# Zero matmuls ahead of TensorE's waits, and rounds counted in registers, in a graph network kernel on one core

## What is computed

```python
x = _layernorm(x + gat(x, src, dst))         # 4 heads: softmax over a node's edges, then a weighted sum
x = _layernorm(x + deviation(x, src, dst))   # standard deviation of the messages of a node
x = _layernorm(x + gine(x, edge_attr, ...))  # sum of x[src] + edge_attr @ We, then an MLP
x = _layernorm(x + sage(x, ...))             # four mean-aggregating layers
```

## Time and profile before

| | |
|---|---|
| median of 3 runs | 11548.31 us |
| profiled execution, its own time and its span | 11566.34 us, 11564.5 us |
| TensorE matmul, weight load | 7105.4 us (61%), 5266.1 us (46%) |
| VectorE, GpSimd, ScalarE | 5149.2 us (45%), 5676.9 us (49%), 1762.4 us (15%) |
| granted TensorE clock, mean | 0.74 |

### The profile page before, as it was taken

The page is one execution under the profiler, slowest core; times in us unless marked ns, Lnnn a source line. Parts: engine busy times, 40 slices in busy tenths (PEclk is TensorE's granted clock), DMA queues, the critical chain, the costliest instruction groups (busy, mean ns, idle before and its releaser), DMA issues.

```text
span 11564.5 us, 251765 instructions
## 1 busy us (share of the span) xinstructions
PE 7105.4 (61%) x60627; PEld 5266.1 (46%) x60628; DVE 5149.2 (45%) x13946; ACT 1762.4 (15%) x3566; POOL 5676.9 (49%) x5555
## 2 busy tenths in 40 slices
PE   5676766664476666778854445455666555555666
PEld 4555555554122112455533344445555444444566
DVE  4555555555887776444322233333322333232333
ACT  2333333332133454000000000000000000000000
POOL 4777756553000001652047777776542765543754
PEclk6777777776888999888965555667777666666777
DMA  2333222221012234555532222224555666555566
GB/s 61 72 72 74 69 67 66 63 62 52 22 67 89 122 133 160 153 152 171 175 88 52 54 57 56 58 59 146 186 183 188 220 223 239 183 183 197 200 221 203
DMA packets 977745, 1416.35 MB, mean 122 GB/s; under 512 B 540705, under 2 KB 649761, under 8 KB 970914
## 3 DMA queue, kind: packets, MB, share of 16 engines
q1 hardware_dynamic: 689858, 1130.79, 28.8%
q0 software_dynamic: 184832, 224.29, 8.9%
q10 hardware_dynamic: 102752, 58.62, 1.7%
HBM read 1197.73 MB, written 215.36 MB: 122 GB/s over the span
## 4 chain that ended last, share of the span: by engine, by line
PE 31%; issue 22%; DVE 16%; DVEq 13%; POOL 12%; DMA 3%; ACT 1%; SPq 0%; POOLq 0%; ACTq 0%
PE ps_turn L934 14%; POOL ARENA L631 12%; PE ps_out L787 6%; PE ps_turn L891 4%; DMA ARENA<-counts 2%; PE ps_pair L787 2%; DVE onehots L1729 2%; DVEq L1743 2%; DVE ARENA L1644 2%; DVE ARENA L1646 2%; PE ps_pair L962 1%; PE ps_turn L703 1%; PE ps_out L707 1%; DVEq L395 1%; DVEq L1651 1%
## 5 line engine op out<-in xcount | busy, mean ns | idle before, releaser
L631 POOL DMA_INDIRECT ARENA<-table_sage,idx x1920 | 1895.3, 987 | 1737.6 <-DVE idx L1724 1198.8
L934 PE MATMUL ps_turn<-ARENA 128*128 128x96 bf16 (+2 forms) x24010 | 2275.5, 263 | 540.5 <-DVE DSUM L1775 216.9
L934 PEld LDWEIGHTS ps_turn<-ARENA 128*128 128x128 bf16 x24010 | 1869.0, 106 | 941.8 <-issue 638.7
L631 POOL DMA_INDIRECT ARENA<-table_gat,idx x1568 | 1743.3, 1112 | 885.4 <-issue 459.8
L631 POOL DMA_INDIRECT ARENA<-table_gine,idx x1568 | 1535.9, 980 | 965.1 <-issue 954.7
L891 PE MATMUL ps_turn<-ARENA 128*128 128x392 bf16 (+1 forms) x4204 | 1067.7, 360 | 667.8 <-DVE ARENA L1646 372.0
L631 POOL DMA_INDIRECT ARENA<-table_dev,idx x480 | 483.6, 1008 | 1753.6 <-DVE idx L1724 1617.3
L962 PE MATMUL ps_pair<-ARENA,onehots 128*128 128x32 bf16 (+2 forms) x10140 | 708.2, 229 | 993.7 <-DVE ARENA L1736 834.5
L787 PE MATMUL ps_out<-ARENA,onehots 128*128 128x256 f32 (+1 forms) x3136 | 937.9, 468 | 510.5 <-DMA ARENA<-table_gine,idx 368.5
L1644 DVE TENSOR_SCALAR ARENA<-ARENA 128x784 bf16<-128x784 f16 (+1 forms) x2102 | 1008.0, 480 | 360.3 <-issue 227.1
L962 PEld LDWEIGHTS ps_pair<-ARENA,onehots 128*128 x10140 | 581.3, 118 | 1126.3 <-issue 1125.2
(11 more groups left out here) (300 smaller groups left out, 6458.9 us busy)
## 6 DMA issues: line engine op xcount, KB each, us to landing
ARENA<-counts SPq DMA_DIRECT2D x1470, 448.0 KB
counts<-ARENA SPq DMA_DIRECT2D x49, 3136.0 KB, 9.0
ARENA<-counts SPq DMA_DIRECT2D x490, 224.0 KB
ARENA<-dst_b SPq DMA_DIRECT2D x393, 256.0 KB
ARENA<-edge_attr SPq DMA_DIRECT2D x390, 128.0 KB, 2.5
ARENA<-table_sage,idx POOLq DMA_INDIRECT x1920
ARENA<-table_gat,idx POOLq DMA_INDIRECT x1568
ARENA<-table_gine,idx POOLq DMA_INDIRECT x1568
```

Source lines behind the costliest of these rows:

```text
L631: pool.indirect_dma_start(ps["buf"][:, s, c, 0:ps["row"]], None, ps["table"][:, :], bass.IndirectOffsetOnAxis(idx[:, s, c:c + 1], 0)).then ...
L934: last = pe.matmul(ps_dense[half][:, 0:n], RING[:, b, :], XP[:, b, :], start=(b == PIECE_AT[pieces[0]]), stop=(j == pieces[-1] and b == PI ...
```

## The change

A helper `fill(n)` issues n matmuls of a 128x128 tile of zeros with 128 columns of zeros into ps_turn columns 1920 to 2048, which nothing reads. In the gat pass 5 of them stand in front of the wait for logit_ready, 5 in front of each wait for nodehot_ready (one for each tile), and 6 in front of the wait for messages_ready: 16 in a group with one tile, 21 with two. Since that strip shares memory with ps_turn, TensorE now also waits, at the end of each of the 14 blocks of the gat pass, until ScalarE has copied the transposed block. In the dense passes the two loads of a unit are replaced by a count in registers, with one load for each step of 7 units; the table has 7 entries in place of 50, and 2 steps fill it in place of 13.

```diff
+        def begin_step(eng, turns, b):
+            gain, share, base, _, upto = turns
+            eng.reg_load([gain], GAINS[0:1, bass.ds(b, 1)])
+            eng.reg_mov(share, 0)
+            eng.reg_mov(base, upto)
+
+        def cold_rounds(eng, turns, r0, cold_round):
-            first = eng.value_load(TURNS[0:1, bass.ds(u, 1)], min_val=0, max_val=ROUNDS)
-            upto = eng.value_load(TURNS[0:1, bass.ds(u + 1, 1)], min_val=0, max_val=ROUNDS)
+            gain, share, base, first, upto = turns
+            eng.reg_mov(first, upto)
+            eng.reg_add(share, share, gain)
+            eng.reg_alu(upto, share, 16, ALU.arith_shift_right)
+            eng.reg_add(upto, upto, base)
+            first, upto = eng.snap(first, min_val=0, max_val=ROUNDS), eng.snap(upto, min_val=0, max_val=ROUNDS)
             with eng.If(first < upto):
...
+            def fill(n):
+                for _ in range(n):
+                    pe.matmul(ps_fill, ZERO[:, :], ZERO[:, :], start=True, stop=True)
...
                 def expand(g, lo, hi):
+                    fill(5)
                     pe.wait_ge(logit_ready, g + 1)
                     pe.matmul(ps_exp_all[:, 0:C * 2 * H], ZERO[:, :], ZERO[:, 0:C * 2 * H], start=True, stop=False)
                     with pe.Fori(lo, hi) as t:
                         pe.reg_add(spread, spread, 1)
+                        fill(5)
                         pe.wait_ge(nodehot_ready, pe.snap(spread, min_val=1, max_val=GROUPS * TILES))
...
                         if gat:
+                            fill(6)
                             pe.wait_ge(messages_ready, g * 2 + 2)
...
                     node_tensor(pe, k, b)
+                    if gat:
+                        pe.wait_ge(step_sem["copied"], block_count("copied", "gat", b))
+                        settle(pe)
...
-                        with pe.Fori(0, KT) as u:
-                            dense_unit(k, u, u + half * KT, SRC_HALF)
+                        with pe.Fori(0, STEPS) as b:
                             if half == 0:
-                                cold_rounds(pe, u, r0, cold_round)
+                                begin_step(pe, turns, b)
+                            with pe.Fori(0, TB) as r:
+                                u = b * TB + r
+                                dense_unit(k, u, u + half * KT, SRC_HALF)
+                                if half == 0:
+                                    cold_rounds(pe, turns, r0, cold_round)
...
-                for r in range(TB):
-                    step(ve.tensor_scalar(shares[:, :, r], gain, float(r * 9363), None, ALU.mult))
...
+                step(ve.tensor_scalar(gain, gain, float(TURN_SHARE), None, ALU.mult))
+                step(ve.tensor_copy(GAINS[:, :], gain))
```

More of the change, by code:

```diff
@@ L50 @@
 ROUND_COLS = SLOTS * C
+TURN_SHARE = (1 << 16) // TB + 1
 AHEAD = 5
@@ L249, in build @@
         INFO = sb("INFO", [P, 2], I32)
-        TURNS = sb("TURNS", [P, KT + 1], I32)
+        GAINS = sb("GAINS", [P, STEPS], I32)
         rangev = sb("rangev", [P, 2 * H])
@@ L321, in build @@
         ps_dense = [ps_turn[:, 1024:1536], ps_turn[:, 1536:2048]]
+        ps_fill = ps_turn[:, 2048 - P:2048]
         ps_out = psum("ps_out", 1024)
@@ L429, in load_four, with turn_registers, begin_turns @@
             return span(eng, spans[s % 4])
-        def cold_rounds(eng, u, r0, cold_round):
-            first = eng.value_load(TURNS[0:1, bass.ds(u, 1)], min_val=0, max_val=ROUNDS)
-            upto = eng.value_load(TURNS[0:1, bass.ds(u + 1, 1)], min_val=0, max_val=ROUNDS)
+        def turn_registers(eng, name):
+            return [eng.alloc_register(f"{name}_{q}") for q in ("turn_gain", "turn_share", "turn_base", "turn_first", "turn_upto")]
+        def begin_turns(eng, turns):
+            eng.reg_mov(turns[4], 0)
+        def begin_step(eng, turns, b):
[10 more added lines that the diff above has]
+            first, upto = eng.snap(first, min_val=0, max_val=ROUNDS), eng.snap(upto, min_val=0, max_val=ROUNDS)
             with eng.If(first < upto):
@@ L919, in _ @@
             arrived = pe.alloc_register("pe_arrived")
+            turns = turn_registers(pe, "pe")
             def dense_unit(k, t, u, srcs):
@@ L968, in pass_dense @@
                 r0 = pe.value_load(INFO[0:1, 0:1], min_val=0, max_val=ROUNDS - 1)
+                begin_turns(pe, turns)
                 if dev:
@@ L1693, in build_vector @@
                 step(ve.tensor_tensor(gain, TARGETS[:, 1:STEPS + 1], TARGETS[:, 0:STEPS], ALU.subtract))
-                shares = tmp[:, 0, 0:KT].rearrange("p (b r) -> p b r", b=STEPS)
-                shares_i = tmp[:, 1, 0:KT].bitcast(I32)
-                for r in range(TB):
-                    step(ve.tensor_scalar(shares[:, :, r], gain, float(r * 9363), None, ALU.mult))
[L1698 to L1703, removed]
+                step(ve.tensor_scalar(gain, gain, float(TURN_SHARE), None, ALU.mult))
+                step(ve.tensor_copy(GAINS[:, :], gain))
                 ve.sem_inc(info_ready, 1)
@@ L1712, in _ @@
             prev, after = ve.alloc_register("ve_prev"), ve.alloc_register("ve_after")
+            turns = turn_registers(ve, "ve")
             def pass_dense(k):
@@ L1720, in pass_dense @@
                 r0 = ve.value_load(INFO[0:1, 0:1], min_val=0, max_val=ROUNDS - 1)
+                begin_turns(ve, turns)
                 def take_indices(s, g):
@@ L1786, in unit @@
                     if rounds:
-                        cold_rounds(ve, t, r0, cold_round)
+                        cold_rounds(ve, turns, r0, cold_round)
                     take_dense(t, u, 1)
@@ L1794, in pass_dense @@
                         step.loop(b, per + 1)
+                        begin_step(ve, turns, b)
                         with ve.Fori(0, TB) as r:
```

## The result

The changed kernel takes 11373.27 us (median of 4 runs, 11365.33 to 11384.98); the kernel before, run beside it, 11557.76 us. The ratio is 0.9843, 95% interval 0.9828 to 0.9858: 1.6% faster, 184 us by the medians. The forecast of 11430 us is 57 us too high; 11373 lies in its range and also inside the range 11350 to 11510 of the likeliest case. The profiled execution took 11374.41 us, its span is 11372.6 us.

The account below looks back on a forecast made before the run. The prediction took chains between engines, read pass by pass, to bound the kernel. Registers were to gain 92 us and fills with the added wait 25, so 117 us off 11548 gives 11430 us, range 11290 to 11550.

Parts of the forecast that it names:

- The bound checks stay: Dense passes, each unit: checks remain when loads go, so 0.5 to 0.85 us come off the sequencer, 0.75 taken.
- A second tile gives 1.8 us (9.86 - 8.03): Gat pass, last stretch: a full clock would save 1.8 us in each of 72 groups with a second tile.
- The fills cost a two-tile group 0.28 us: Gat pass, two-tile groups: only the first 5 fills count, 0.28 us each group, for 71 late groups.
- One-tile groups pay 0.65 us and gain 0.4: Gat pass, one-tile groups: fills expose 0.65 us, full clock gives some 0.4 us on average.
- The clock stays low for about one group after each round: Gat pass, after round ends: 24 late and 12 middle rounds at 2 us take back 48 and 24 us.
- The middle stretch loses 5 us: Gat pass, the 98 groups after the first 100: fills cost about 45 us against 40 gained from the clock.
- The added wait costs 12 us: Gat pass, block ends: schedule and span loads end about 1 us too late in 12 blocks, 12 us.
- rival 1: Gat pass: fills hardly cost and the clock stays up across round ends; 11221 us, halfway there 11300; chance 15%.
- rival 2: Gat pass: fills are the bound, as TensorE is already late in one-tile groups; 108 us lost, 11656 us; chance 7%.
- rival 3: Dense passes: the ring at its limit hides the register gain, 35 us in place of 92; 11490 us; chance 10%.
- rival 4: TensorE's unrolled round grows by 256 instructions, the jump back must fetch code; 100 us lost, 11530 or more; chance 5%.
- rival 5: Gat pass: zeros or narrow work don't raise the clock; fills cost 140 us and gain nothing; 11608 us; chance 5%.

Follow-up runs that it names:

- e1: The changed kernel without any fills and without the added wait, registers alone: 11420.81 us against 11556.05 of the kernel before, ratio 0.9879.
- e3: The kernel before with both table loads per unit kept and the check behind each load dropped: 11509.7 us, ratio 0.9958 to the kernel before.
- e2: The kernel before with the fills and the added wait, its two table loads per unit kept: 11517.04 us, ratio 0.9961 to the kernel before.
- e5: The changed kernel with 10, 10 and 12 fills in place of 5, 5 and 6: 11525.65 us, ratio 0.9969 to the kernel before.
- e4: The changed kernel with the wait for copied moved behind the two schedule loads of the next block: 11368.02 us, ratio 0.9831 to the kernel before.
- e7: The changed kernel with 44 fills more behind the last aggregation of a gat round: 11434.11 us, ratio 0.9893 to the kernel before.
- e9: The changed kernel without fills in a round's first group, on a chip where the kernel before takes 15010.92 us: ratio 1.0035 to the kernel before.
- e11: The changed kernel without the six fills before messages_ready, on a chip where the kernel before takes 15010.92 us: ratio 0.9995 to the kernel before.
- e6: The changed kernel with as many fills, each one column in place of 128: 11440.56 us, ratio 0.9898 to the kernel before.
- e12: The changed kernel, copied wait behind the schedule loads, no fills before nodehot_ready or in a round's first group: 11383.73 us, ratio 0.9846 to the kernel before.

## Why the prediction was right, and where its steps were not

The direction and the order of the parts were right; the sum was 67 us short (the forecast only 57, as the kernel before measured 9 us higher this time), 43 of them in Part 1 and 14 in Part 2; 10 are the scatter between the kernels' medians. That Part 2 came out near its 25 us is luck: estimated from the groups below, the clock's gain was put some 86 us too high in the last stretch (72 x 1.2) and the fills' cost some 65 (108 x 0.6), and the two cancel.

**Part 1, registers: mis-sized, 92 us forecast and 135 measured (e1), above its upper bound of 115.** The step that failed is "The bound checks stay". They didn't, and in the trace of before they were a third of the way: e3 puts them at 0.51 us a unit on the sequencer and 46 us of time. Without that step the count is 1.21 us a unit (1.55 - 0.34) where 0.75 was taken. By the profiled executions, whose spans differ by 146 us and not 135, sage1 and sage4 gained 107 us in e1 against 63; 2 x 42 x 1.21 is 102. No wait for counts appeared in either, so that sign of being wrong stayed away. Sage2 and sage3 gained 30 against 22 (2 x 15 x 1.21 = 36), and as forecast little between units: in these two passes TensorE's waits for counts grew from 73 to 179 us. Dev gained 6 against 10, the build's end 2.8 against 2.

The prediction weighed a figure of the Trainium skill (DMA: Bandwidth & Descriptors, Latency and other measured facts) of about 600 ns for a load, which would have made the part 150 us. The total came out nearer to that than to 92, but not for its reason: the loads of one register measured 0.306 us in e3 as they did before.

**Part 2, fills: 25 us forecast, 39 measured (e2), two errors of opposite sign.**

- *The first 100 groups gain nothing:* right. With twice the fills (e5) they still take 556 us: the gathers cover them.
- *A second tile gives 1.8 us (9.86 - 8.03):* right for a group at such a clock, wrong for all 72. The earlier trace rows compared two different groups, but another trace of the same code shows the second of them at full clock: what took 9.86 us at 0.76 in the kernel before takes 8.04 at 1.00 in e1 (first line), which has no fills either, and 9.92 at 0.77 in e3 (second line; columns as in the earlier trace rows).

```profile
2430.07:2438.11 8.04, 6.53 (x81) 5.51 (x78) 4.26 (x13) 2.11 (x6) 6.21 (x7) 1.00 0.30 59
```

```profile
2431.74:2441.66 9.92, 8.42 (x71) 6.78 (x71) 4.26 (x13) 2.10 (x6) 7.09 (x7) 0.77 0.28 55
```

  What was wrong is the count. In mid-round the 46 two-tile groups had a mean clock of 0.88 before (0.97 after), and only 15 of them were below 0.80: 15 x 1.8 is 27 us, 0.6 for each of the 46. They gained 0.31 us each, fills paid ((368.7 - 354.3) / 46), where gain less cost was to be 1.5.
- *The fills cost a two-tile group 0.28 us:* right. In 14 such groups that stand at full clock (0.99 or more) both before and after, the time grew by 0.29 us on average. The one that took 8.03 us takes 8.61, the one of 9.86 takes 8.83, and one of 9.83 (at 0.94) takes 9.84. Before, then three times after:

```profile
2111.20:2121.03 9.83, 8.05 (x85) 6.86 (x86) 4.49 (x13) 2.11 (x6) 7.70 (x8) 0.94 0.22 51
```

```profile
2078.43:2088.27 9.84, 9.13 (x111) 7.53 (x107) 4.27 (x12) 2.11 (x6) 7.40 (x9) 1.00 0.24 53
2383.59:2392.20 8.61, 7.45 (x90) 6.06 (x89) 4.28 (x13) 2.11 (x6) 6.78 (x7) 0.99 0.24 58
```

```profile
2395.92:2404.75 8.83, 8.06 (x107) 6.87 (x105) 4.29 (x12) 2.11 (x6) 6.70 (x8) 1.00 0.26 58
```

- *One-tile groups pay 0.65 us and gain 0.4:* the cost is wrong. In 14 one-tile groups of mid-round that stand at full clock both before and after, the 16 fills cost 0.05 us on average and nothing in the median: nearly all of them fit into time that TensorE had. All 75 gained 0.26 us net ((345.1 - 325.9) / 75), as their mean clock went from 0.77 to 0.94, so the clock gave about 0.3. The second set of 16 in e5 found no such room: 0.61 us in the 56 that are at full clock in both kernels.
- *The clock stays low for about one group after each round:* right. In slot 0 of the last stretch it is 0.60 (0.59 before), in slot 1 0.82, in slots 2 to 6 0.91 to 0.98. The 24 first groups grew by 15 us, 13 of them behind a block.
- *The middle stretch loses 5 us:* it gained 12.8. With a mid-round balance of +0.26 in place of -0.25 for a one-tile group this follows for 52 such groups (10.2 of the 12.8 by their own sum).
- *The added wait costs 12 us:* 7 in e4, by a start 1.3 us later at 12 blocks. Mechanism right.

**Rivals.** 1 (11300 or less): no, though e7 shows that a round end can be bridged as far as the clock goes. 2: no in the changed kernel; e5 stands 1.3% above it, and 52 of its 137 us in gat lie in the first groups behind a block, where the jump is not covered. 3: its mechanism holds in sage2 and sage3; on the chip of e9 to e11 most of the gain is missing, but waits for counts didn't take it. 4: not in the changed kernel, where the jumps are 0.21 us, but real in e5 and e7, where the groups behind a block lose 52 and 39 us. 5: no (e6).

A slip of arithmetic: halfway from 11430 to rival 1's 11221 is 11326, not the 11300 and 11290 that stand there. The measured time lies above all three.

**Open.** The groups at full clock in two traces are those that reach it by themselves, so the costs of 0.05 and 0.29 us may not hold for the others. Why e12 isn't the sum of its parts was not settled, nor whether a bridge of so few fills that the block's jump stays short would gain.

## What to carry to other kernels

Before you price a table read in a sequencer, list all rows between the read and its use: here the loads with their address steps were nearly half of the way and the bound checks another third, and registers with declared bounds leave no row at all. Work that only keeps the clock up pays where an engine is late and its clock low, costs whatever doesn't fit into its waits (0.05 us a group here and 0.29 there, 0.61 more with twice as much), and adds code: look at the loop's jump back (0.21 or 3.7 us) before and after. To price a clock, compare the same group of the same code in two traces, at two clocks; then count how many groups stand at the low one before you multiply.

## What the runs showed that was not expected

- A bound check behind a loaded value costs 0.26 us of a sequencer (0.51 for two, e3); an asserted range on a register that was computed costs nothing.
- Fills of one column leave the clock at 0.77 where 128 columns give 0.85, with the same number of matmuls and of weight loads (e6).
- The jump back of a loop went from 0.21 to 3.6 us with 44 matmuls more in the unrolled round for the outer loop (e7), and to 3.7 with 128 more for the inner one as well (e5).
- The same group of the same code stood at clock 0.76 in one trace and at 1.00 in another, and took 9.86 and 8.04 us.
- On one chip the same kernel took 15011 us in place of 11558, with GpSimd's waits for index lists grown from 406 to 1356 us.
